# Placement in a routed feed-forward kernel: four slot-tile one-hots by one VectorE comparison, and token numbers carried by the row one-hots

## What is computed

```python
scores = jax.nn.softmax(xf @ Wg, axis=-1)
weights, indices = jax.lax.top_k(scores, TOP_K)        # TOP_K = 4 of E = 32 experts
...
C = CAP_FACTOR * P // E
for e in range(E):
    pos = jnp.nonzero(pair_expert == e, size=C, fill_value=P)[0]
    valid = pos < P
    safe = jnp.minimum(pos, P - 1)
    tok = jnp.where(valid, pair_token[safe], 0)
    ...
    out = swiglu(xf[tok], W1[e], W2[e], W3[e]) * w[:, None]
    y = y.at[tok].add(out)
...
x = x + 0.5 * ffn(layernorm(x)); x = x + attn(layernorm(x)); x = x + 0.5 * ffn(layernorm(x))
```

## Time and profile before

| | us |
|---|---|
| median of the timed runs | 3153.11 (3 runs, 3150.93 to 3154.76) |
| the profiled execution | 3140.06 |
| its span, first to last instruction | 3138.3 |
| placement loop, layer 0 (90.1 to 133.2 us) | 43.1 |
| placement loop, layer 1 (2610.5 to 2651.1 us) | 40.6 |
| busy, whole span: PE, ACT, DVE, POOL | 2749.7, 2275.9, 2074.5, 730.2 |

### The profile page before, as it was taken

The page is one execution under the profiler, slowest core; times in us unless marked ns, Lnnn a source line. Parts: engine busy times, 40 slices in busy tenths (PEclk is TensorE's granted clock), DMA queues, the critical chain, the costliest instruction groups (busy, mean ns, idle before and its releaser), DMA issues. The chain is left out here.

```text
span 3138.3 us, 59917 instructions
## 1 busy us (share of the span) xinstructions
PE 2749.7 (88%) x16843; PEld 1092.2 (35%) x16844; DVE 2074.5 (66%) x3847; ACT 2275.9 (73%) x3449; POOL 730.2 (23%) x902
## 2 busy tenths in 40 slices
PE   5599977868999999999999999999999775999754
PEld 5388744431222212222212222212121162887432
DVE  5744436656877868778677786868778667444245
ACT  2644423448999999999999999999999725444200
POOL 5455545512000000000000000000000044555565
PEclk9999988889999999999999999999999985999876
DMA  5555453421001001010010010010000035555533
GB/s 158 150 155 156 146 111 103 116 81 24 5 3 25 3 3 26 3 19 10 4 25 3 5 24 5 3 23 4 3 4 3 21 105 172 157 155 146 113 109 108
DMA packets 132049, 195.29 MB, mean 62 GB/s; under 512 B 22364, under 2 KB 99324, under 8 KB 130428
## 3 DMA queue, kind: packets, MB, share of 16 engines
q1 hardware_dynamic: 104188, 117.00, 13.3%
q0 software_dynamic: 27648, 75.53, 9.7%
HBM read 124.85 MB, written 67.50 MB: 61 GB/s over the span
## 5 line engine op out<-in xcount | busy, mean ns | idle before, releaser
L1632 ACT ACTIVATE RB<-psS 128x1024 f32<-128x1024 f32 x1920 | 1765.8, 1215 | 7.9 <-PE psS L1550 7.9
L1584 PE MATMUL psO<-RB,values 128*32 128x512 f32 x7680 | 1025.5, 606 | 0.5 <-ACT RB L1632 0.5
L1550 PE MATMUL psS<-WE 51*128 51x512 f16 x3840 | 695.5, 387 | 80.2 <-DMA WE<-shift_d 11.0
L1550 PEld LDWEIGHTS psS<-WE 51*128 51x128 f16 x3840 | 174.8, 93 | 1094.1 <-ACT RB L1632 1071.7
L638 POOL DMA_INDIRECT xg<-xn_d,index x320 | 304.8, 953 | 227.0 <-issue 197.0
L662 PE MATMUL psH<-WE,xgt 128*128 x1280 | 341.3, 389 | 2.1 <-DVE xgt L706 2.1
L1503 POOL COPY values<-WE 128x512 f32 x12 | 7.0, 611 | 1318.0 <-PE psO L1584 1318.0
L726 ACT ACTIVATE gate<-psH 128x128 f32<-128x128 f32 x320 | 88.7, 277 | 247.2 <-PE psH L662 244.7
L711 DVE TENSOR_TENSOR hid<-gate,psH 128x128 f32<-128x128 f32 x320 | 92.1, 288 | 258.7 <-ACT gate L726 229.9
L1584 PEld LDWEIGHTS psO<-RB,values 128*32 128x32 f32 x7680 | 151.3, 108 | 276.9 <-issue 246.9
L1648 DVE TENSOR_SCALAR part<-psO 128x512 f32<-128x512 f32 x256 | 172.1, 672 | 108.4 <-PE psO L1550 108.4
(11 more groups left out here) (243 smaller groups left out, 3204.4 us busy)
## 6 DMA issues: line engine op xcount, KB each, us to landing
pair_d<-ob SPq DMA_DIRECT2D x320, 128.0 KB
WE<-part_d SPq DMA_DIRECT2D x84, 128.0 KB
xn_d<-ws SPq DMA_DIRECT2D x64, 128.0 KB, 1.7
WE<-in_W SPq DMA_DIRECT2D x2, 4096.0 KB, 23.5
part_d<-raw SPq DMA_DIRECT2D x32, 256.0 KB, 2.6
xg<-xn_d,index POOLq DMA_INDIRECT x320
RA<-in_x SPq DMA_DIRECT2D x8, 512.0 KB, 7.7
head_d<-sums SPq DMA_DIRECT2D x128, 32.0 KB, 1.6
```

The costliest lines, as they stand in the source:

```text
L1550: return pe.matmul(ps, K[r][rows, kt * P:(kt + 1) * P], Q[r][rows, at:at + BLK], start=True, stop=True)
L1584: last = pe.matmul(psO[g % 2][32 * j:32 * (j + 1), :], values[:, r, j % 2, kt, :], weights, start=(kt == 0), stop=(kt == KT - 1))
L1632: act.activation(probs[n % RING][:, half * 2 * BLK:(half + 1) * 2 * BLK], psS[m % HELD][:, :], ACT.Exp, scale=SCALE).then_inc(sem("exped"), 1)
```

## The change

The tile one-hots no longer carry the token number; the row one-hots do. So all four tile one-hots of a token tile are a plain comparison, and one `tensor_tensor` of 640 elements makes them, of `iota_h` and a new fp16 copy `hi_h` of the tile numbers, both broadcast. The numbers must be exact in fp16, so they now run from 1 to 2048 in each half of the tokens, and the two halves accumulate in two halves of `psI` (columns 0 to 159 and 160 to 319). After the loop four DVE operations join the halves, where one was.

The makers of row one-hots multiply by the number: POOL by a second operation and a second scalar, fetched from the new `pool_row`; DVE by the number's column; ACT by giving the Relu the scale `-number` (`neg_number`, made ahead of the loop) and the bias `number`, which yields number x Relu(1 - apart). ACT's two Relus of a token tile become one of 256 elements, and each maker waits once a token tile for its buffers.

```diff
@@ consts @@
-        zrow = sb(f"zrow{L}", [P, NJ], F16, c)
+        zrow = sb(f"zrow{L}", [P, 2 * NJ], F16, c)
...
-                pool.iota(number_i[:, :], pattern=[[P, NT]], base=-T // 2, channel_multiplier=1).then_inc(sem("consts"), 1)
+                pool.iota(number_i[:, :], pattern=[[0, 2], [P, NT // 2]], base=1, channel_multiplier=1).then_inc(sem("consts"), 1)
@@ POOL @@
-                    pool.tensor_copy(lo_now[:, :, :], lo_f[:, bass.ds(i * 2, 2), 0:1]).then_inc(sem("row_fetched"), 1)
+                    pool.tensor_copy(lo_now[:, :, :], pool_row[:, bass.ds(i * 2, 2), :]).then_inc(sem("row_fetched"), 1)
...
-                        pool.tensor_scalar(at_row[:, w * TOPK, :], iota_h[:, 0:P], lo_now[:, w, :], None,
-                                           ALU.is_equal).then_inc(sem("row_onehot"), 1)
+                        pool.tensor_scalar(at_row[:, w * TOPK, :], iota_h[:, 0:P], lo_now[:, w, 0:1], lo_now[:, w, 1:2],
+                                           ALU.is_equal, ALU.mult).then_inc(sem("row_onehot"), 1)
@@ ACT @@
                     for w in range(2):
+                        act.wait_ge(sem("act_onehot"), i * 2 + (w + 1))
                         for k in range(TOPK // 2):
-                            act.wait_ge(sem("act_onehot"), i * TOPK + (w * (TOPK // 2) + k + 1))
-                            act.activation(apart[:, w * (TOPK // 2) + k, :], iota_h[:, 0:P], ACT.Abs, bias=neg_lo[:, bass.ds(i * 2 + w, 1), k + TOPK // 2])\
+                            act.activation(apart[:, w, k, :], iota_h[:, 0:P], ACT.Abs, bias=neg_lo[:, bass.ds(i * 2 + w, 1), k + TOPK // 2])\
                                .then_inc(sem("apart"), 1)
-                        for k in range(TOPK // 2):
-                            b = w * TOPK + TOPK // 2 + k
-                            act.wait_ge(sem("apart"), i * TOPK + (w * (TOPK // 2) + k + 1))
-                            act.wait_ge(sem("placed"), i * (2 * TOPK) + (b + 1))
-                            carried(act, sem("seen_act"))
-                            act.activation(at_row[:, b, :], apart[:, w * (TOPK // 2) + k, :], ACT.Relu, scale=-1.0, bias=one[:, :])\
-                               .then_inc(sem("act_onehot"), 1)
+                        act.wait_ge(sem("apart"), i * TOPK + (w + 1) * (TOPK // 2))
+                        act.wait_ge(sem("placed"), i * (2 * TOPK) + (w + 1) * TOPK)
+                        carried(act, sem("seen_act"))
+                        act.activation(at_row[:, w * TOPK + TOPK // 2:(w + 1) * TOPK, :], apart[:, w, :, :], ACT.Relu,
+                                       scale=neg_number[:, bass.ds(i * 2 + w, 1)], bias=number[:, bass.ds(i * 2 + w, 1)])\
+                           .then_inc(sem("act_onehot"), 1)
@@ PE @@
                 for t in range(NT):
+                    half = slice(t // (NT // 2) * NJ, (t // (NT // 2) + 1) * NJ)
                     for k in range(TOPK):
                         b = t % 2 * TOPK + k
-                        pe.wait_ge(sem("onehot"), t * TOPK + (k + 1))
                         if k == 0:
+                            pe.wait_ge(sem("tile_onehot"), t + 1)
                             pe.wait_ge(sem("row_onehot"), t + 2)
-                        elif k >= TOPK // 2:
-                            pe.wait_ge(sem("act_onehot"), t * (TOPK // 2) + (k - TOPK // 2) + 1 + TOPK)
-                        pe.matmul(psI[:, 0:NJ], at_row[:, b, :], at_tile[:, b, :],
+                        elif k == 1:
+                            pe.wait_ge(sem("onehot"), t + 1)
+                        elif k == 2:
+                            pe.wait_ge(sem("act_onehot"), t + 3)
+                        pe.matmul(psI[:, half], at_row[:, b, :], at_tile[:, b, :],
                                   start=False, stop=False, skip_group_check=True).then_inc(sem("placed"), 1)
-                pe.matmul(psI[:, 0:NJ], zeros[:, :], zrow[:, :], start=False, stop=True).then_inc(sem("all_placed"), 1)
+                pe.matmul(psI[:, 0:2 * NJ], zeros[:, :], zrow[:, :], start=False, stop=True).then_inc(sem("all_placed"), 1)
@@ DVE @@
-                link(v.tensor_tensor(hi_f[:, :, :], hi_f[:, :, :], pv[:, :, :], ALU.add))
+                mark(v.tensor_scalar(neg_number[:, :], number[:, :], -1.0, None, ALU.mult))
+                mark(v.tensor_copy(pool_row[:, :, 0], lo_f[:, :, 0]))
+                mark(v.tensor_copy(pool_row[:, :, 1], number[:, :]))
+                link(v.tensor_tensor(hi_h[:, :, :], hi_f[:, :, :], pv[:, :, :], ALU.add))
...
                     for w in range(2):
-                        for k in range(TOPK):
-                            t, b = i * 2 + w, w * TOPK + k
-                            v.wait_ge(sem("placed"), i * (2 * TOPK) + (b + 1))
-                            if k == 1:
-                                v.tensor_scalar(at_row[:, b, :], iota_h[:, 0:P], lo_f[:, bass.ds(t, 1), k], None, ALU.is_equal)
-                            v.tensor_scalar(at_tile[:, b, :], iota_h[:, :], hi_f[:, bass.ds(t, 1), k], number[:, bass.ds(t, 1)],
-                                            ALU.is_equal, ALU.mult).then_inc(sem("onehot"), 1)
+                        t = i * 2 + w
+                        v.wait_ge(sem("placed"), i * (2 * TOPK) + (w + 1) * TOPK)
+                        v.tensor_tensor(at_tile[:, w * TOPK:(w + 1) * TOPK, :], iota_h[:, :].unsqueeze(1).to_broadcast([P, TOPK, NJ]),
+                                        hi_h[:, bass.ds(t, 1), :].rearrange("p a k -> p (a k)").unsqueeze(2).to_broadcast([P, TOPK, NJ]),
+                                        ALU.is_equal).then_inc(sem("tile_onehot"), 1)
+                        v.tensor_scalar(at_row[:, w * TOPK + 1, :], iota_h[:, 0:P], lo_f[:, bass.ds(t, 1), 1], number[:, bass.ds(t, 1)],
+                                        ALU.is_equal, ALU.mult).then_inc(sem("onehot"), 1)
...
-                link(v.tensor_scalar(tok_f[:, :], psI[:, 0:NJ], float(T // 2), None, ALU.add))
+                link(v.tensor_scalar(later[:, :], psI[:, NJ:2 * NJ], 0.5, float(T // 2 - 1), ALU.is_gt, ALU.mult))
+                link(v.tensor_tensor(later[:, :], later[:, :], psI[:, NJ:2 * NJ], ALU.add))
+                link(v.tensor_scalar(tok_f[:, :], psI[:, 0:NJ], -1.0, 0.0, ALU.add, ALU.max))
+                link(v.tensor_tensor(tok_f[:, :], tok_f[:, :], later[:, :], ALU.add))
                 link(v.tensor_copy(slot_token[:, 0:NJ], tok_f[:, :]))
```

12 lines of the change are left out of this document (8 added, 4 removed).

## The result

| | before | after |
|---|---|---|
| median of five timed runs, us | 3154.03 (3150.93 to 3155.56) | 3175.78 (3174.03 to 3189.26) |
| profiled execution, us | 3140.06 | 3174.03 |
| its span, us | 3138.3 | 3171.7 |

The ratio is 1.0075 with a 95% interval of [1.006, 1.009]: the kernel became slower by 0.75%, some 22 us. The prediction was 3165 us with a range to 3177. The sign is right and the time lies inside the range, but the step from before was put at 12 us and is nearly twice that. So the question is where the other 10 us come from, and whether the engine that the prediction named sets the pace.

The account below looks back on a forecast made before the run. The prediction took the two placement loops, paced by ACT, to bound the kernel. Loops +9.1 us plus 3.2 us ahead of and behind them gave +12.3 us on the 3153.11 us median: 3165 us, range 3155 to 3177.

Parts of the forecast that it names:

- up to 0.3 us more a tile costs nothing: POOL in the loop: second operation and four-number fetch fit in its 0.64 us of idle time.
- ACT's chain: Placement loops: merged Relu waits bare for both Abs, 1.45 us a tile, 92.8 us against 83.7, 9.1 us more.
- 1.37 to 1.62 us a tile: Band for ACT's tile time in the loops, upper part for slow fetches: +7 to +23 us, held at 75%.
- loops alike in both layers: Sign in the profile after: both placement loops at about 47 us each.
- POOL with more idle time than now: Sign in the profile after: DVE and POOL both idle longer in the loops than before.
- POOL rows of over 1 us: Sign in the profile after that would show the lock between DVE and POOL.
- What bounds the kernel before: Both placement loops, 83.7 us, move the end one for one; ACT paces them, 1.265 us a tile, 1.347 in layer 0.
- POOL is shut out: Rival, 6%: DVE's long comparison holds up POOL's row one-hot each time, 1.77 us a tile, total 3186 us.
- DVE's comparison: Loop: one tensor_tensor of 640 elements takes 0.82 us, other bound some 0.5 for two-byte data; off the path.
- The row one-hot on DVE: Loop: about 0.25 us a tile, as one at_tile comparison before; off the path.
- Behind the loop: Between last matmul and slot_token: three more DVE operations 1.07 us, larger closing matmul 0.1 us, per layer.
- Ahead of the loop: Before lo_ready: three small DVE operations (neg_number, two copies into pool_row), 0.4 us on the path in each layer.

Follow-up runs that it names:

- b3_act_ahead: Kernel before with ACT's Relus merged (scale -1, bias one) and the next tile's Abs pair issued ahead of this tile's Relu: ratio 1.001, loops 42.05 and 37.94 us.
- a4: Changed kernel with POOL out of the loop, DVE making the row one-hot of k = 0 too: ratio 1.0069, loops 49.30 and 47.56 us.
- b2_pool_op: Kernel before with a second operation and second scalar (times one) on POOL's row one-hot: ratio 1.0, loops 43.49 and 40.88 us.
- a2: Kernel before with one long tensor_tensor comparison for the four tile one-hots, token number left out: loops 45.55 and 45.66 us, whole ratio 1.0154 not comparable.
- a3: Changed kernel with four plain tensor_scalar comparisons in place of the one tensor_tensor: ratio 1.0071, loops 49.31 and 47.56 us.
- f_after_pe64: Changed kernel with 64 idle semaphore increments on PE ahead of each placement loop: ratio 1.0046, loops 50.00 us, experts of layer 1 4.3 us shorter.
- a1: Kernel before with ACT's merged Relu alone, scale and bias from register-addressed vectors of -1 and 1: ratio 1.0066, loops 49.37 and 47.62 us.

## Why the prediction was right in sign and wrong about the pace

The step that failed is the one on POOL: "up to 0.3 us more a tile costs nothing". By the prediction ACT's chain sets the loop at 1.45 us a tile and POOL has room. The runs show a loop set by POOL at 1.563 us a tile, with ACT's chain a little below it (1.486 to 1.541). That the time still fell inside the range is luck: the forecast's 1.37 to 1.62 us a tile were meant for ACT's chain with slow fetches, and took in POOL's pace by chance. The sign that was to show ACT's chain, loops alike in both layers, came true for POOL's reason; of the other signs, "POOL with more idle time than now" failed, and POOL rows of over 1 us, named as the sign of the lock, came.

- **What bounds the kernel before: right, with one error.** The loops move the end about one for one: the stages' sum and the step of the medians agree to 1 us, on two chips. But the 0.08 us a tile by which layer 0 was slower is no property of the pace; idle increments in ACT's program take most of it away.
- **ACT's chain, 1.45 us a tile: right in kind, short by 0.04 in layer 1.** The Relu lasts 0.600 us (I said 0.58): the second vector is 0.09 us, as taken, and the 128 further elements are 0.11 us and not 0.10 (507 ns in b3_act_ahead for 393). It starts 0.28 us behind the Abs, as 0.20 + 0.08. In sum 0.68 + 0.28 + 0.60 less an overlap of 0.09 is 1.47, and a4 shows 1.486 with the branch. In layer 0 it is 1.541. That makes 97 us for the two loops where I had 92.8 (12.5 us more than before's 84.4 for my 9.1), a term mis-sized by 3.4 us. I had put such slower fetches into the range, not into the sum.
- **On POOL, "up to 0.3 us more a tile costs nothing": this step failed.** It was an allowance that I never filled. The second operation alone takes 0.2 us of it, which b2_pool_op shows to be free by itself. The wait for DVE's comparison takes 0.3 more on the mean row one-hot, and the fetch lengthens by 0.25. POOL then needs 1.56 us a tile, more than ACT, and the loops are 3.2 us longer than ACT would make them.
- **The rival "POOL is shut out" (6%): right in mechanism, its price too high.** It said 1.77 us a tile, since every row one-hot would wait for a whole comparison. Measured is 1.563, since a quarter begin outside one (784 ns) and the others inside, on the way through it (1.06 to 1.44 us). It also left out the second operation's 0.2 us; with that its price would have been 1.97. I held against it that DVE's four at_tile went across POOL's 0.62 us. That was a row about another instruction: one tensor and two scalars, 0.3 us each. It says little of one comparison of 0.83 us between two tensors. a2 is the proof, since there POOL's own instruction is unchanged. Whether the second tensor or the length makes the difference isn't shown; a3's short comparisons of one tensor cost POOL 0.15 us on the mean. The Trainium skill, "SBUF — State Buffer", section "Terms", has the pair share its ports by an exclusive lock held for the full instruction; for POOL behind a comparison the trace agrees (the fetch ends 0.05 us behind it, all 48 row one-hots at 0.72 to 0.75). For a comparison that begins inside a row one-hot it shows 0.09 us more, and no wait of the 0.58 us that the one-hot still runs. For the four-instruction stream of before it shows POOL slowed by little, 589 ns at the least and 633 on the mean.
- **DVE's comparison: right,** 0.826 us for 0.82; the bound of 0.5 for two-byte data fell. **The row one-hot on DVE** takes 0.31 us for 0.25, off the path.
- **Behind the loop: right.** The three more operations and the closing matmul were 1.17 us a layer; the tail grew by 1.20. The timeline of the kernel after, layer 0, answers to the earlier trace rows:

```profile
141.58 0.47 PE L481 MATMUL psI<-zrow,zeros 128*128 128x320 f16 x1
142.16 0.33 DVE L609 TENSOR_SCALAR later<-psI 128x160 f32<-128x160 f32 x1 [1.50 <-PE psI L481]
142.52 0.32 DVE L610 TENSOR_TENSOR later<-later,psI 128x160 f32<-128x160 f32 x1
...
143.60 0.24 DVE L613 CAST slot_token<-tok_f 128x160 int32<-128x160 f32 x1
```

- **Ahead of the loop:** 0.26 us for 0.4. The three operations have 32 elements, not 128, and follow 0.10 us apart.
- **A term that was missing:** PE's shorter program. I said of PE only that it has the same 128 matmuls, and the experts of layer 1 lost 4 us (299.5 for 295.4; on another chip 6.6, 298.5 for about 292). That the shorter program does it is shown by f_after_pe64; why isn't.

Of the gap of some 10 us, about 3.4 are by this count ACT's chain, 3.2 POOL beyond it, and 4 PE's program. Had ACT's chain been as cheap as I put it, POOL would have set the same 50.0 us, and its share of the gap would be 6.5.

## What to carry to other kernels

When two short operations that cover each other's waits are merged, price the bare wait, and get it covered by work of the next round before you merge (in layer 1 b3 gained 2.9 us where a1's bare merge, with register-addressed vectors, lost 6.7). An allowance for an engine "off the path" must be filled in with every addition, and a long two-tensor operation on DVE was here an addition to POOL. Compare the stages that an edit doesn't touch as well: a fifth of this result came from there.

## What was unexpected of the hardware

- A two-tensor comparison of 640 two-byte elements on DVE (0.83 us) holds POOL up: a copy of four numbers takes 0.19 us beside none and up to 0.85 inside one, a row one-hot 0.78 and up to 1.44. All 48 row one-hots that begin inside one end 0.72 to 0.75 us behind it. A comparison that begins inside a row one-hot loses only 0.09 us.
- A second operation with a second per-partition scalar costs POOL 0.20 us for 128 elements (589 to 791 ns at the least), and a second per-partition vector costs ACT 0.09 us (393 to 485 ns).
- Idle increments in a program change the time of what comes behind them: 64 on PE take 4.3 us off the experts of layer 1, 32 take 9 us off attention in one kernel and nothing in another, and 4 or 24 on ACT take 1.4 to 1.7 us off a loop of 32 token tiles.
